# One attention remainder set between two maxima, and four expert weights a step later

## The reference

```python
x = x + tanh(g_xattn) * xattn(layernorm(x), ctx)     # 16 heads of 64, rope on q and k
x = x + tanh(g_ffn) * ffn(layernorm(x))              # 2 shared experts, 16 routed, top 4

# xattn
scores = einsum('bhqd,bhkd->bhqk', qh, kh) * DH ** (-0.5)
window_mask = (j <= i) & (j >= i - W)                # W = 64
probs = softmax(where(window_mask, scores, -1e30))
out = einsum('bhqk,bhkd->bhqd', probs, vh);  return out @ wo.T
# ffn
act = gelu(einsum('th,reh->tre', xt, routed_up)) * gate[:, :, None]
routed = einsum('tre,rhe->th', act, routed_down)
```

## Time and profile before

| | us |
|---|---|
| three runs | 507.98, 508.57, 509.18 |
| median | 508.57 |
| the profiled execution, its own time | 510.26 |
| its span in the trace | 508.4 |

### The profile page before, as it was taken

One profiled execution on the slowest core, in us unless ns is written; L12 is line 12 of the kernel. 1 busy time (PEld: TensorE's weight loads), 2 busy tenths in 40 slices (PEclk: granted clock), 3 DMA queues, 4 the chain that ended last, 5 costly groups with the idle time before them and its releaser, 6 DMA issues.

```text
span 508.4 us, 14340 instructions
## 1 busy us (share of the span) xinstructions
PE 495.0 (97%) x5386; PEld 406.8 (80%) x5386; DVE 358.9 (71%) x1159; ACT 310.8 (61%) x861; POOL 266.0 (52%) x206
## 2 busy tenths in 40 slices
PE   8998999999999999999999999999999999999997
PEld 5787798888888888887788788778878887888885
DVE  5998958756797667868777767796657565745454
ACT  4597685566766665856766775766456545644442
POOL 3899999999998999997788411001000100000000
PEclk9999999999999999999999999999999999999999
DMA  7462214230132310310310247316802491255021
GB/s 256 129 204 63 62 38 142 64 80 19 35 109 48 93 37 4 79 39 23 81 39 23 60 136 265 101 26 171 250 14 31 114 297 18 32 164 221 0 35 50
DMA packets 50996, 46.37 MB, mean 91 GB/s; under 512 B 30224, under 2 KB 33424, under 8 KB 50928
## 3 DMA queue, kind: packets, MB, share of 16 engines
q1 hardware_dynamic: 50928, 45.46, 31.7%
HBM read 32.72 MB, written 2.24 MB: 69 GB/s over the span
## 4 chain that ended last, share of the span: by engine, by line
PE 77%; POOL 10%; DVE 5%; issue 4%; ACT 2%; DMA 1%; DVEq 0%; SPq 0%; POOLq 0%; ACTq 0%
PE ring L1191 54%; PE psS L1191 10%; PE psTO L1421 5%; PE psS L1382 3%; POOL prob L562 3%; POOL arena L549 2%; PE psTO L1402 2%; POOL arena L554 2%; PE psS L1208 1%; PE psTO L1398 1%; DVE arena L917 1%; POOL arena L543 1%; POOL wl L570 1%; DVE arena L914 1%; DVE arena L1084 1%
## 5 line engine op out<-in xcount | busy, mean ns | idle before, releaser
L1191 PE MATMUL ring<-xTh,wh 128*128 128x512 f32 x268 | 108.2, 404 | 0.5 <-DVE arena L917 0.2
L1191 PE MATMUL ring<-xTh,wl 128*128 128x512 f32 x268 | 105.3, 393 | 0.0
L1191 PE MATMUL ring<-xTl,wh 128*128 128x512 f32 x268 | 105.1, 392 | 0.0
L562 POOL TENSOR_TENSOR prob<-prob,rinv 128x512 f32<-128x512 f32 x62 | 66.1, 1070 | 17.8 <-DVE rinv L1094 17.5
L675 ACT ACTIVATE oTh<-prob 128x512 fp32r<-128x512 f32 x64 | 40.4, 631 | 54.4 <-PE ring L1191 26.8
L987 DVE TENSOR_TENSOR oTl<-prob,oTh 128x512 fp32r<-128x512 f32 x64 | 44.1, 689 | 37.1 <-ACT oTh L675 36.6
L659 ACT ACTIVATE sneg<-ring 128x512 f32<-128x512 f32 x72 | 42.8, 595 | 33.1 <-PE ring L1191 33.0
L596 POOL TENSOR_TENSOR rstd<-vare,mhalf 128x4 f32<-128x4 f32 x8 | 9.2, 1156 | 102.8 <-DVE vare L884 102.8
L979 DVE TENSOR_TENSOR prob<-sneg,arena 128x512 f32<-128x512 f32 x64 | 44.2, 690 | 24.8 <-ACT sneg L659 24.8
L1191 PEld LDWEIGHTS ring<-xTh,wh 128*128 128x128 f32 x268 | 50.3, 188 | 12.6 <-issue 0.9
L1191 PEld LDWEIGHTS ring<-xTh,wl 128*128 128x128 f32 x268 | 50.3, 188 | 11.2
(11 more groups left out here) (146 smaller groups left out, 1172.0 us busy)
## 6 DMA issues: line engine op xcount, KB each, us to landing
arena<-gate_scratch SPq DMA_DIRECT2D x64, 256.0 KB, 6.2
raw<-in_e SPq DMA_DIRECT2D x18, 256.0 KB, 2.7
raw<-in_w SPq DMA_DIRECT2D x16, 256.0 KB, 3.7
arena<-arena SPq DMA_DIRECT2D x24, 128.0 KB, 2.3
pT<-pT SPq DMA_DIRECT2D x96, 32.0 KB, 2.0
arena<-arena SPq DMA_DIRECT2D x10, 256.0 KB, 3.4
out<-x SPq DMA_DIRECT2D x16, 128.0 KB, 6.0
x<-in_x SPq DMA_DIRECT2D x3, 512.0 KB, 4.5
```

Source lines behind the costliest of these rows:

```text
L562: pool.tensor_tensor(prob[:, c % BUFS, :, :], prob[:, c % BUFS, :, :], rinv[:, c % BUFS, :].unsqueeze(2).to_broadcast([P, TT, P]), ALU.mul ...
L1191: last = pe.matmul(out, a, b, start=start and i == 0 and j == 0, stop=stop and i == n - 1 and j == 2, skip_group_check=check)
```

## The change

Two edits.

In 14 steps, those with k = 2 from 6 to 58, `rest_att` on DVE now stands between the maxima of the two heads; before, it stood behind both maxima and the reciprocal. The remainder of these steps is the last one that the output product y of the next step waits for. In the steps with k = 0 its place is unchanged.

The weights 16, 17, 18 and 20 move from steps 41, 45, 49 and 53 (k = 1) to 42, 46, 50 and 54 (k = 2), with everything that their job does on ACT, DVE and SP.

```diff
-WEIGHT_STEPS = {6: 11, 7: 12, 8: 13, 11: 14, 12: 15, 41: 16, 45: 17, 49: 18, 51: 19, 53: 20, 55: 21}
+WEIGHT_STEPS = {6: 11, 7: 12, 8: 13, 11: 14, 12: 15, 42: 16, 46: 17, 50: 18, 51: 19, 54: 20, 55: 21}
...
                     score_max(c)
+                    if c % G == 2:
+                        rest_att(attended[c])
                     score_max(c + 1)
                 if OPENED < c < CLOSING - 1 and not before_q(c - 1):
                     invert(c - 1)
-                if c in attended:
+                if c in attended and c % G != 2:
                     rest_att(attended[c])
```

## The result

| | before | after |
|---|---|---|
| time, median of 6 and 6 runs | 509.37 us (507.98 to 510.79) | 505.67 us (505.17 to 506.35) |
| profiled execution: span, time | 508.4, 510.26 us | 503.4, 505.21 us |

The ratio is **0.9931, with an interval of 0.9913 to 0.9948**. Against the earlier median of before, 508.57, the gain is 2.9 us; against all six runs of before (those three and three later ones), 3.7. The forecast was 506.3, a gain of 2.2.

What follows compares the result with a forecast made beforehand. POOL was taken to bound the attention's opening and PE 87 to 205 us, with PE's remainder waits to win; 2.28 + 0.1 - 0.15 = 2.2 us off 508.57 gave 506.3 us, range 504.4 to 508.1.

Steps and rivals of the forecast that it cites:

- PE at 87 us: Sign of being wrong: PE at 87 us more than 0.5 us earlier or later than in the kernel before.
- a shift's landing: Sign of being wrong: the landing of a DMA shift of the values carries the difference in time.
- values that wait for ACT in steps 48, 52 and 56: Sign of being wrong: PE's values product in these steps waits for ACT.
- Three times 0.76 in steps 46, 50 and 54: Output products no longer wait for the attention remainder, 0.76 us each; gain 2.28 us.
- The thin cover of 0.05 us on ACT: Steps 46, 50, 54: the weight's 0.62 us rounding fits ahead of ACT's second copy, 0.05 us over.
- The rival in which ACT's copies bound all four steps: ACT's second copy slips by the whole rounding, no gain to speak of, 508.5 us, 507.5 with half; chance 0.2.
- Step 42: ACT, also rounding the next sequence's x, is already the limit; gain 0.1 us, bounds 0 and 0.76.
- Step 6: Opening: the remainder wait goes, but POOL's division starts late and idle time takes the 1.04 us back; loss 0.15 us.
- The DMA wait: At 247.16 us step 52's values waited 1.26 us for a shift; no gain taken, up to 1.3 us possible.
- The slower rival, more late shifts: Shifts of the values land late more often, each costing 1.3 us; three more give 510.3 us; chance 0.05.
- The other interleaved steps: Ten steps with the interleaved remainder and no wait before: nothing won, nothing lost.
- The inner range: The forecast's own range, 505.4 to 507.2 us, with step 42 and the opening at their bounds; chance 0.61.

Runs made afterwards that it cites:

- e8: The changed kernel with weight 16 in step 38 instead of 42; 505.19 us beside 509.15 for the kernel before, ratio 0.9921.
- e2: The kernel before with only the interleaving, the remainder between the two heads' maxima, weights where they were; 508.2 us beside 509.0, ratio 0.998.
- e4: The kernel before with weights 16, 17 and 20 moved, 18 left in step 49, no interleaving; 508.12 us, ratio 0.9977 to the kernel before.
- e9: The kernel before with only SP's part of weight 18 moved behind the jobs of step 50; 509.2 us beside 508.88, ratio 1.0.
- e1: The kernel before with only the four weights moved a step later, the remainder behind both heads; 506.49 us beside 509.0, ratio 0.9943.
- e11: e10 with weight 19 in step 52 instead of 51; 506.01 us, ratio 0.9948 to the kernel before.
- e10: The changed kernel with step 6's remainder behind both heads as before and weight 16 in step 38; 505.47 us beside 508.88, ratio 0.993.
- e12: The kernel before with the opening's idle products cut into 18 instead of 5, same 2560 columns; 510.43 us beside 509.24, ratio 1.0025.

## Why the prediction was right, and where it was off

The time, the sign and the range held, in part by luck: the gain by the traces, without the opening, is 3.6 us, and the forecast 2.2, while the median of before, from which it was counted, rose by 0.8 with the later runs. Two of the prediction's own signs of being wrong came: PE at 87 us is 1.4 us earlier (85.66 in after, by the opening alone), and a shift's landing carries 1.34 us of the difference. The third, values that wait for ACT in steps 48, 52 and 56, did not. By the steps of the sum:

**Three times 0.76 in steps 46, 50 and 54: as forecast.** The products start at T+0.35, and the values come 0.74 and 0.72 earlier in steps 48 and 56; of the 2.09 in step 52, the 1.34 of the DMA taken off, 0.75 is left. The thin cover of 0.05 us on ACT held: in after the second copy of step 51 had no idle time in front of it (241.82, above), and the values started at 4.72, not at 5.3. The rival in which ACT's copies bound all four steps is refuted for these three.

**Step 42: 0.1 forecast, 0.22 measured, for the reason given.** The values now wait for ACT, as the timeline of after says by name:

```profile
208.19 1.15 PE L1423 MATMUL psTO<-pT,arena 128*64 128x64 f32 x32 [0.54 <-ACT pT L778]
```

e8 takes the rounding out of that step and gets the remaining 0.6 us, all of ACT's rounding.

**Step 6: -0.15 forecast, 0.0 measured.** The mechanism held: the wait for the remainder is gone, and the scores of step 8 wait that much longer. After, the opening, to be read beside the earlier trace rows:

```profile
43.26 0.60 PE L1404 MATMUL psTO<-ident,prob 128*128 128x128 f32 x4
...
43.74 0.36 PE L1193 MATMUL ring<-wh,oTh 128*128 128x256 f32 x1
...
44.35 0.17 DVE L1094 RECIPROCAL rinv<-rsum 128x4 f32<-128x4 f32 x1
...
44.44 0.66 DVE L1004 TENSOR_TENSOR wl<-raw,wh 128x512 fp32r<-128x512 f32 x1
...
44.60 1.40 POOL L562 TENSOR_TENSOR prob<-prob,rinv 128x512 f32<-128x512 f32 x1 [0.15 <-DVE rinv L1094]
...
49.03 0.99 PE L1384 MATMUL psS<-arena 64*32 64x96 f32 x64 [1.67 <-issue]
```

From T to the scores it is 5.77 us (49.03 - 43.26), and it was 5.76 (50.41 - 44.65): the 0.9 us won at the product are idle time in front of the scores. POOL has 0.15 us of idle time in front of its division, as forecast, and the division starts 0.20 later against T; but it takes 1.40 and not 1.60, and ends at T+2.74 both times (44.60 + 1.40 - 43.26; 45.79 + 1.60 - 44.65), 0.90 behind the end of the weight's remainder in both. T of step 7 to T of step 11 took 21.06 and 21.07. The forecast passed the division's later start on to its end; but in both kernels the end follows that of the remainder, T+1.84. That the pair is slow together, as the prediction has it, is a misreading: the remainder took 0.69 there, its usual time, and only the division was slow. The profile's word for the wait was "issue"; it was a chain through POOL.

**The DMA wait: zero forecast, 1.34 measured. This is the term that was mis-sized**, and it is nearly all of the distance between the forecast gain of 2.2 and the measured 3.6; the other differences, 0.12 in step 42, 0.15 in step 6, 0.16 between T of step 11 and T of step 35, -0.07 in the three steps of 0.76, -0.27 in step 54 and -0.06 in the rest, nearly cancel. I wrote that "in another execution the landing may be an ordinary one". It was not an accident of one execution: e2, e4 and e9 had it too, one trace each, and in no kernel with weight 18 moved did the values of step 52 wait for it. I also argued from SP's order alone, that the load stood ahead of the shift; e9 shows that this order does nothing to the landing. What I did not look at was the third part of the DMA view, which shows one instruction packet in the very microsecond of the slow issue. The slower rival, more late shifts, had the right point from which it decides but not the cause: which copy meets a packet depends on the code and its timing, and the change could as well have brought such a meeting about. Its chance of 0.05 was rather low for that.

**Not forecast: a new loss of 0.27 in step 54.** PE and, ahead of it, ACT in after:

```profile
251.45 1.15 PE L1423 MATMUL psTO<-pT,arena 128*64 128x64 f32 x32 [0.20 <-ACT pT L778]
...
246.26 0.40 ACT L760 ACTIVATE prob<-sneg,nmax 128x128 f32<-128x128 f32 x1 [1.83 <-DVE nmax L1084]
```

With weight 18 in step 50, DVE has its remainder, the norm's sums, the addition of an output and weight 19's remainder in a row, and the maxima of step 52 come late; ACT waits 1.83 us for them, and its copies for step 54 slip past what PE needs. e1 has the same late stretch to 0.01 us, so the interleaving does not cause it. That DVE's row does is argued from the timeline: e11, which takes weight 19 out of it, won 0.10 from T of step 51 to T of step 55 (17.38 against 17.48 in e10) and lost more in step 55, so the runs bear out 0.10 of the 0.27 at most, and the rest is open.

**The other interleaved steps: nothing, as forecast.** (They are nine, not ten: 14 less steps 6, 42, 46, 50 and 54.) T of step 11 to T of step 35 took 104.24 in before, 104.08 in after and 104.0 to 104.5 in the others, with either order.

**The inner range.** The forecast's own range, 505.4 to 507.2, does not follow from the bounds that it names: with step 42 and the opening at their bounds the sum gives 504.5 to 506.8. The measured 505.67 lies in both.

## What to carry to other kernels

A wait on the critical engine is worth what the next late thing leaves of it: 0.74 where ACT had room, 0.22 where it had none, and nothing where POOL was the chain; the trace of before told all three. When a DMA lands late in one place only, look for instruction packets in the two microseconds behind its issue before calling it chance; a few instructions more or less early in the program can create or remove such a meeting, so a small gain from any edit may be this and not the edit. When DVE and POOL start within hundredths of a microsecond of each other, as in step 6, a difference of 0.1 us between two kernels may be only who went first; set the edited trace against several of the old order and not one. When an edit is tried in parts, read each part by a stretch of the trace between two fixed points, since here the opening alone varied by 1.5 us.

## What the runs showed of the hardware

A 16 KB instruction packet kept one DMA engine busy for 0.9 to 1.6 us over all the traces, 1.0 of it in e12 (3.2% x 16 x 2 us) and 1.39 in step 50 of before. Of 123 DMA issues on SP that overlapped one, 32 took over 0.8 and up to 1.9 us, where 0.3 to 0.7 is usual. A copy of L404 or L407 that had one begin 1.3 to 1.4 us after its issue landed in 3.4 to 4.0 us and not in 2.0 to 2.4, ten times of ten. In e9 another packet began in the issue of a DMA at 172.80 (1.49 us), and PE then stood 0.53 us on "issue" at 175.49; that the two belong together is argued, not shown.

DVE and POOL on each other's heels: a weight's remainder of 512 columns took 0.68 alone, 1.16 when it began 1.78 us into a POOL instruction of 2.40, and 1.99 when it began 0.96 us into one of 2.39: in both of these cases it ended about 0.55 us after POOL did. When the two started within 0.04 us of each other, in step 6, either POOL's division was quick (1.04) and the remainder slow (1.56 to 1.58), six times, or the division slow (1.59 to 1.60) and the remainder quick (0.67 to 0.69), four times.
